# Late numerator sums added by a DMA, squares of six blocks added by GpSimd, in a kernel with an interleaved first phase

## The chip, the cores and the metric

One core of one Trainium2 chip. The metric is the device time of one execution in microseconds; the kernel before takes 4677.09 us (median of 3 runs, 4675.98 to 4685.37). In the text PE is TensorE, DVE is VectorE, ACT is ScalarE, POOL is GpSimd, and SP is the engine that only issues DMAs.

## The reference

Two layers over `x` of shape (4, 1024, 1024), float32. The part around the change is the first operation of each layer, a bidirectional decaying scan along the sequence, with the same `k = v = side` in both layers:

```python
decay = exp(-exp(w)) * (0.5 + 0.5 * tf)
ek = exp(minimum(k, 30)); ekv = ek * v
# a = a*decay + ekv, b = b*decay + ek, forward (nf, df) and backward (nb, db)
euk = exp(minimum(u + k, 30))
num = nf + nb - ekv + euk * v
den = df + db - ek + euk
out = sigmoid(r) * num / maximum(den, 1e-8) * (0.8 + 0.2 * tf)
```

Layer 0 then does `x + out @ (W * scale).T + bias`. Layer 1 adds its own scan result, and then an RMS norm (mean of squares over the 1024 channels), a router with the top 4 of 32 experts, a shared expert (`silu(h @ sg) * (h @ su) @ sd`) and the routed experts.

## The kernel before

The scans work on blocks: 128 channels (partitions) by 1024 positions. There are 32 blocks (4 batches of 8), and a **unit** is the work of one block for both layers, `l = 0` and `l = 1`. A unit leaves two tiles in DRAM: `gated` (layer 0, times sigmoid(x)) and `ratio` (layer 1).

The matmuls of layer 0, the norm and the shared expert work on **halves**: 512 positions of all 8 channel blocks. There are 8 halves, `h` = 0 to 7, of 32 **steps** each. A step is one 128-row product of 24 matmuls (operands are split in a high and a low float32r part, three matmuls per pair). Steps 0 to 15 make layer 0 and, in between, the down products of the half before; from step 16 on stand gate and up products. Between product 15 and product 16 lies the **normalisation**: every block has to be multiplied by the inverse root of the mean of squares before PE can go on.

The order is written out by hand in `with_halves`, the same for every engine. Units 0 to 7 run alone (while PE and ACT split the weights), and the last of them carries the first loads of half 0. After that half `h` (0 to 5) is interleaved with units 8+4h to 11+4h, eight steps in each: the unit calls `fill(0)` to `fill(7)` at its own places, and `fill` does what its engine has to do for that step. Halves 6 and 7 have no units. Then come the experts, a loop over some 150 tiles of 128 tokens, which is 57% of the span.

What the prediction follows, with lines of the kernel before:

- **Numerator.** DVE makes `W = min(euk, cap) * side` (L980), scans `G` forward (L972) and backward (L983). In units 0 to 7 PE adds the two in PSUM (L1421, L1426). In all later units DVE adds them, `G = G + W` (L988). DVE then makes the inverse in two Newton steps (L996, L998, both into `W`), multiplies (L1002, into `N`) and, for `l = 0`, multiplies by the sigmoid (L1007), which counts `gated` up.
- **The next unit's side tile.** ACT waits for `gated`, issues the store of `gated` (L719) and behind it, on the same queue, the load of the next unit's side tile (L665, `load_side`). When it has landed POOL clips it at 30 into `EK` (L595, `clip`, counts `kc`), and ACT takes the exponential (L660, `side_exp`), after `inverse(1)` and before `fill(6)`.
- **Squares.** ACT squares block `o` of the half into the one tile `SQ` (L785, at step `SQUARE_AT[o]`), and PE adds it up with a matmul against a tile of ones in `SUM_BANK` (L1467, at step `SUM_AT[o]`), 8 times per half. ACT can't write the next square before PE has read the last.
- **Steps 13 to 15.** PE transposes the half before's output block 4 into `OUT_BANK` (L1493), ACT copies it to `RS` (L768, in `fill(6)` of the second unit, right behind `side_exp`), SP stores `RS` (behind product 14, on which its queue waits), and only then can ACT copy block 5 (L768, `fill(7)`) and take logarithm and exponential of the sums (L793, L795). DVE refines the root (L1253 to L1261) and scales the first block (L1270), and PE starts the transposes of the normalisation (L1477). The transposes of output block 5 on PE wait for ACT's copy of block 4.

```python
SQUARE_AT = (3, 4, 5, 7, 9, 11, 13, 13)
SUM_AT = (5, 5, 6, 8, 10, 12, 13, 14)
COPY_AT = (6, 8, 10, 12, 14, 15, 17, 18)
R_AT = 2 * CB - 1
```

## Time and profile before

| | us |
|---|---|
| median of 3 runs (lowest, highest) | 4677.09 (4675.98, 4685.37) |
| span of the profiled execution | 4682.9 |
| PE busy | 4475.7 (96%) |
| DVE busy | 2567.2 (55%) |
| ACT busy | 1789.8 (38%) |
| POOL busy | 722.8 (15%) |

No time of the profiled execution is given besides its span, which is 5.8 us over the median of the runs. Busy time of PE is modelled: each matmul is shown longer than the distance to the next, so a PE that looks busy may still be paced by gaps; distances between starts are what the reader should take. Busy shares of the whole span mix five stages with different limits, so the stages are read one by one: the units alone (to about 311 us), half 0 up to its normalisation (to 404), the rest of the interleaved halves (to 1545), halves 6 and 7 (to 2003), and the experts.

### The profile page before, as it was taken

The numbers are of one execution on the slowest core, as the hardware profiler recorded it, in microseconds if no ns is written. First come the engines' busy times: TensorE is split into PE (matmuls) and PEld (weight loads), VectorE is DVE, ScalarE is ACT, GpSimd is POOL, SyncE is SP. The second block draws the span as 40 slices with busy tenths as digits, with TensorE's granted clock in tenths as the row PEclk, the third lists the DMA queues.
The fourth block names the chain that finished last, engine by engine and source line by source line (L and its number), as shares of the span: only waits on it lengthen the run. The fifth ranks groups of instructions, "written<-read, shape, count | busy, mean of one in ns | idle before, by whom it ended". The sixth has DMA issues, their size and how long they took to land.

```text
span 4682.9 us, 60901 instructions
## 1 busy us (share of the span) xinstructions
PE 4475.7 (96%) x19862; PEld 3545.7 (76%) x19863; DVE 2567.2 (55%) x2765; ACT 1789.8 (38%) x2596; POOL 722.8 (15%) x934
## 2 busy tenths in 40 slices
PE   6777999999999999999999999999999999999998
PEld 2245877777777877878888888888888888888887
DVE  8999999999999653433233434444341253333432
ACT  5665555555555333232222323334231142222321
POOL 1000000000000017211111112112111121111111
PEclk8888999999999999999999999999999999999999
DMA  6675767767676766754344545555552254444543
GB/s 226 235 263 184 274 241 268 251 223 282 240 268 226 270 212 190 251 182 111 95 131 112 170 112 160 171 166 150 182 168 57 61 186 145 112 112 116 161 109 61
DMA packets 247928, 835.08 MB, mean 178 GB/s; under 512 B 28160, under 2 KB 61056, under 8 KB 222976
## 3 DMA queue, kind: packets, MB, share of 16 engines
q1 hardware_dynamic: 172944, 572.77, 34.5%
q0 software_dynamic: 47728, 160.07, 15.5%
q10 hardware_dynamic: 27136, 100.67, 5.8%
q8 instruction: 72, 1.18, 0.1%
q14 instruction: 48, 0.39, 0.0%
HBM read 652.40 MB, written 181.01 MB: 178 GB/s over the span
## 4 chain that ended last, share of the span: by engine, by line
PE 80%; DVE 10%; issue 4%; ACT 3%; DMA 2%; POOL 0%; ACTq 0%; DVEq 0%; POOLq 0%; SPq 0%
PE ps L1593 34%; PE ps L1457 22%; PE ps L1607 16%; PE ps L1526 3%; PE ps L1479 1%; PE ps L1582 1%; DVE work L969 1%; DVE work L975 1%; DMA work<-rows_dram,row_idx 1%; PE ps L1477 1%; PE ps L1467 1%; DVE work L996 1%; DVE work L998 1%; DVE work L972 1%; DVE work L1002 1%
## 5 line engine op out<-in xcount | busy, mean ns | idle before, releaser
L1593 PE MATMUL ps<-halves 128*128 128x512 f32 x7152 | 1698.6, 393 | 3.5 <-DVE halves L1356 2.8
L1593 PEld LDWEIGHTS ps<-halves 128*128 128x128 f32 x7152 | 1338.5, 189 | 279.9 <-DVE halves L1356 3.1
L1457 PE MATMUL ps<-halves 128*128 128x512 f32 x6144 | 1450.2, 395 | 13.7 <-issue 12.5
L1457 PEld LDWEIGHTS ps<-halves 128*128 128x128 f32 x6144 | 1154.1, 189 | 287.2 <-issue 47.8
L1607 PE MATMUL ps<-halves 128*128 128x512 f32 x3576 | 834.9, 389 | 1.3 <-DVE halves L1372 1.3
L1607 PEld LDWEIGHTS ps<-halves 128*128 128x128 f32 x3576 | 671.1, 188 | 140.9 <-DVE halves L1372 1.6
L1356 DVE TENSOR_TENSOR halves<-ps,halves 128x1024 fp32r<-128x1024 f32 x150 | 183.7, 1225 | 905.2 <-ACT halves L852 905.2
L1351 DVE TENSOR_TENSOR halves<-work,halves 128x1024 fp32r<-128x1024 f32 (+1 forms) x320 | 440.2, 1433 | 83.6 <-ACT halves L856 83.3
L852 ACT ACTIVATE halves<-ps 128x1024 fp32r<-128x1024 f32 x150 | 154.0, 1027 | 862.4 <-PE ps L1593 862.4
L576 POOL DMA_INDIRECT out<-work,add_idx x149 | 249.8, 1677 | 1417.3 <-DVE work L1378 1382.2
L856 ACT ACTIVATE halves<-work 128x1024 fp32r<-128x1024 f32 (+1 forms) x320 | 369.1, 1229 | 67.0 <-PE ps L1607 56.5
L1372 DVE TENSOR_TENSOR halves<-ps,halves 128x256 fp32r<-128x256 f32 x298 | 112.4, 419 | 491.7 <-ACT halves L884 491.7
L595 POOL TENSOR_SCALAR work<-work 128x1024 f32<-128x1024 f32 x33 | 106.5, 3226 | 1419.9 <-DMA work<-side_t 1419.9
L884 ACT ACTIVATE halves<-ps 128x256 fp32r<-128x256 f32 x298 | 98.5, 382 | 544.4 <-PE ps L1582 544.4
L1378 DVE TENSOR_SCALAR work<-ps,acc 128x512 f32<-128x512 f32 x149 | 111.6, 749 | 276.4 <-PE ps L1607 266.5
L890 ACT ACTIVATE work<-ps,acc 128x512 f32<-128x512 f32 x149 | 102.1, 685 | 408.5 <-PE ps L1607 388.5
L566 POOL DMA_INDIRECT work<-rows_dram,row_idx x151 | 152.5, 1010 | 123.4 <-POOL row_idx L562 69.0
L1526 PE MATMUL ps<-ident,work 128*128 128x128 f32 x1200 | 157.6, 275 | 12.4 <-DMA work<-rows_dram,row_idx 12.4
L975 DVE TENSOR_TENSOR_SCAN work<-decay,edge_in,work 128x1024 f32<-128x1024 f32 x64 | 154.2, 2409 | 14.2 <-ACT edge_in L680 14.2
L1435 PE MATMUL ps<-plain,ident 128*128 128x512 f32 x128 | 83.0, 736 | 73.6 <-ACT halves L735 73.6
L983 DVE TENSOR_TENSOR_SCAN work<-decay,edge_in,work 128x1024 f32<-128x1024 f32 x64 | 150.7, 2355 | 0.0
L1526 PEld LDWEIGHTS ps<-ident,work 128*128 128x128 f32 x1200 | 137.1, 142 | 13.4 <-DMA work<-rows_dram,row_idx 13.3
(186 smaller groups left out, 3674.4 us busy)
## 6 DMA issues: line engine op xcount, KB each, us to landing
halves<-split_dram SPq DMA_DIRECT2D x512, 512.0 KB, 5.6
work<-expert_w SPq DMA_DIRECT2D x192, 1024.0 KB, 5.5
split_dram<-halves ACTq DMA_DIRECT2D x32, 1024.0 KB, 4.9
plain<-shared_w SPq DMA_DIRECT2D x32, 512.0 KB, 3.2
gated_dram<-work ACTq DMA_DIRECT2D x32, 512.0 KB, 4.1
work<-side_t ACTq DMA_DIRECT2D x32, 512.0 KB, 5.6
work<-x_t ACTq DMA_DIRECT2D x32, 512.0 KB, 3.7
ratio_dram<-work ACTq DMA_DIRECT2D x32, 512.0 KB, 4.2
```

Source lines behind the costliest of these rows:

```text
L566: pool.indirect_dma_start(hx, None, rows_dram[:, :], bass.IndirectOffsetOnAxis(row_idx[:, :].bitcast(u32), 0)).then_inc(s["rows_in"], 16)
L576: pool.indirect_dma_start(out[:, :], bass.IndirectOffsetOnAxis(add_idx[:, :].bitcast(u32), 0), y, None, compute_op=ALU.add).then_inc(s["y_ ...
L852: sc.activation(xhi, ps_xt[:, :], ACT.Copy).then_inc(s["x_hi"], 1)
L856: sc.activation(whi[q][:, part], staged(q, part), ACT.Copy).then_inc(s["w1_hi" if q < 4 else "w2_hi"], 1)
L975: ve.tensor_tensor_scan(F[:, ::-1], d, F[:, ::-1], edge_in[:, 0:1], ALU.mult, ALU.add).then_inc(s["h_bwd"], 1)
L983: ve.tensor_tensor_scan(G[:, ::-1], d, G[:, ::-1], edge_in[:, 1:2], ALU.mult, ALU.add).then_inc(s["nb"], 1)
L1351: ve.tensor_tensor(wlo[q][:, part], staged(q, part), whi[q][:, part].bitcast(f32), ALU.subtract)\
L1356: ve.tensor_tensor(xlo, ps_xt[:, :], xhi.bitcast(f32), ALU.subtract).then_inc(s["x_lo"], 1)
L1457: last = pe.matmul(bank(k % 4), w, op[:, part], start=(c == 0 and w is w_hi and op is hi), stop=(c == CB - 1 and w is w_lo))
L1526: last = pe.transpose(ps_xt[:, c * P:(c + 1) * P], hx[:, c * P:(c + 1) * P], ident[:, :])
L1593: last = pe.matmul(ps_h[:, a * 512:a * 512 + 512], xp[:, xk * P:(xk + 1) * P], wp[:, rhs], start=(xk == 0 and xp is xhi and wp is whi[q]), ...
L1607: last = pe.matmul(ps_y[:, h * 512:h * 512 + 512], ap_[:, (q * 2 + k) * P:(q * 2 + k + 1) * P], wp[:, rhs:rhs + 512], start=(q == 0 and k ...
```

## The change

1. `second`, three more tiles of 1024 columns, gives `W`, `F` and `G` one copy for each layer (`W_of[l]`, `F_of[l]`, `G_of[l]`). The Newton steps now write `F`, the product writes `W`, and `gated` and `ratio` are stored from there. `N` holds the inverse alone.
2. In units 8 to 31, but for 15, 23 and 31 (`prompt`), the numerator is added by a DMA that POOL issues, SBUF to SBUF with accumulation, 512 KB each, 42 in all. The product that needs it is made later (`scaled_late`): for `l = 0` behind the backward scan of `l = 1`, for `l = 1` in the next unit behind its first backward scan.
3. ACT's `store_gated`, with `load_side` in it, stands behind `fill(4)` and so behind the late product; the third and seventh `fill` come after the Newton steps on DVE, `fill(4)` between the scans of `l = 1`.
4. In halves 0 to 6 (`folded`) the square of block 0 goes to `R`, and POOL adds the squares of blocks 1 to 5 to it. PE sums three tiles: `R`, and the squares of blocks 6 and 7. Half 7 keeps its eight.
5. `SCRATCH`: the space for software DMA descriptors is 4096 bytes per partition instead of 16384.

```diff
+        second = sb("second", 3 * SEQ)
+        W_of, F_of, G_of = ((first, second[:, i * SEQ:(i + 1) * SEQ]) for i, first in enumerate((W, F, G)))
...
+        def prompt(u):
+            return u % CB == CB - 1
...
+            def add_numerator(u, l):
+                n = u * 2 + l
+                pool.wait_ge(s["wv_done"], n + 1)
+                pool.wait_ge(s["nb"], n + 1)
+                pool.dma_start(G_of[l], W_of[l], accum_op=ALU.add).then_inc(s["num_added"], 16)
+            def fold_square(h, o):
+                pool.wait_ge(s["sq"], h * CB + (o + 1))
+                if o > 1:
+                    pool.wait_ge(s["sq_folded"], h * (FOLDED - 1) + (o - 1))
+                apart(pool)
+                pool.tensor_tensor(R, R, SQ, ALU.add).then_inc(s["sq_folded"], 1)
...
+                if q == 1:
+                    fold_square(h, 4)
+                if not prompt(u):
+                    add_numerator(u, 0)
+                if q == 0:
+                    fold_square(h, 1)
+                    fold_square(h, 2)
+                if q == 1:
+                    fold_square(h, 5)
+                clip(u + 1, (u + 1) % 2)
+                if not prompt(u):
+                    add_numerator(u, 1)
+                if q == 0:
+                    fold_square(h, 3)
...
                 fill(2)
                 fill(3)
-                sc.wait_ge(s["gated"], u + 2)
-                sc.dma_start(gated_dram[ds(u * P, P), :], N).then_inc(s["gated_out"], 16)
-                load_side(u + 1, 1 - par)
-                fill(4)
+                if prompt:
+                    store_gated()
+                    fill(4)
                 edges(1)
                 euk(1)
+                if not prompt:
+                    fill(4)
+                    store_gated()
                 fill(5)
                 inverse(1)
                 side_exp(u + 1)
                 fill(6)
...
+                    if l == 1 and not prompt:
+                        fill(4)
                     ve.wait_ge(s["h_fwd"], n + 1)
                     ve.wait_ge(s["h_edge"], n + 1)
                     ve.tensor_tensor_scan(F[:, ::-1], d, F[:, ::-1], edge_in[:, 0:1], ALU.mult, ALU.add).then_inc(s["h_bwd"], 1)
+                    if l == 1 and not prompt:
+                        scaled_late(u, 0)
                     fill(4 * l + 1)
+                    if l == 0 and pending:
+                        scaled_late(u - 1, 1)
...
-                pe.matmul(SUM_BANK, ones[:, :], SQ, start=(o == 0), stop=(o == CB - 1)).then_inc(s["sums"], 1)
+                pe.matmul(SUM_BANK, ones[:, :], R if folded(h) and o == first else SQ, start=(o == first), stop=(o == CB - 1))\
+                    .then_inc(s["sums"], 1)
...
-    nc = bacc.Bacc("TRN2", target_bir_lowering=False, num_devices=1)
+    nc = bacc.Bacc("TRN2", target_bir_lowering=False, num_devices=1, dynamic_dma_scratch_size=SCRATCH)
```

How the order moves, at two places of the second unit of half 2 (the other halves read alike). On DVE before, from the second Newton step of `l = 0` to the backward scan of `l = 1` (L1002 is the product, L1007 the gated product, L1291 and L1298 belong to `fill(4)`):

```order
L998 SCALAR_TENSOR_TENSOR work<-work 128x1024 [waits newton1]
L1002 SCALAR_TENSOR_TENSOR work<-work,neg_gain 128x1024 [waits newton2]
L1007 TENSOR_TENSOR work<-work 128x1024 [waits sig_x,gated_raw]
L1291 TENSOR_TENSOR plain<-work 128x512 [waits rl_in0,sig1]
L1298 SCALAR_TENSOR_TENSOR work<-ps,lsb,work 128x512 [waits xl_in3,product]
L969 SCALAR_TENSOR_TENSOR work<-decay,work 128x1024
L972 SCALAR_TENSOR_TENSOR work<-decay,work 128x1024
L975 SCALAR_TENSOR_TENSOR work<-decay,edge_in,work 128x1024 [waits h_edge,h_fwd]
```

The same stretch in the changed kernel (L1080 is the second Newton step, L1048, L1051 and L1056 the scans, L1379 the `fill(3)` that stood before the Newton steps, L1027 and L1032 product and gated product):

```order
L1080 SCALAR_TENSOR_TENSOR work<-work 128x1024 [waits newton1]
L1379 SCALAR_TENSOR_TENSOR work<-ps,lsb,work 128x512 [waits xl_in2,product]
L1048 SCALAR_TENSOR_TENSOR second<-decay,work 128x1024 [waits newton2]
L1051 SCALAR_TENSOR_TENSOR second<-decay,work 128x1024
L1372 TENSOR_TENSOR plain<-work 128x512 [waits rl_in0,sig1]
L1379 SCALAR_TENSOR_TENSOR work<-ps,lsb,work 128x512 [waits xl_in3,product]
L1056 SCALAR_TENSOR_TENSOR second<-decay,edge_in,second 128x1024 [waits h_edge,h_fwd]
L1027 SCALAR_TENSOR_TENSOR work<-work,neg_gain 128x1024 [waits num_added]
L1032 TENSOR_TENSOR work<-work 128x1024 [waits sig_x,gated_raw]
```

The gated product has moved behind three scans and two `fill`s. On ACT before, from the store of `gated` to the logarithm of the sums (L665 loads the side tile, L660 is `side_exp`, L768 the copies of output blocks):

```order
L719 DMA gated_dram<-work 128x1024 [waits gated]
L665 DMA work<-side_t 128x1024 [waits gated]
...
L785 ACTIVATE work<-plain 128x512 [waits sums,c1] x2
L697 ACTIVATE work<-work,neg_low 128x1024 [waits h_all]
L704 ACTIVATE work<-work,low 128x1024 [waits den,gated_out]
L670 DMA work<-x_t 128x1024 [waits wv_done]
L708 ACTIVATE work<-work 128x1024 [waits g_ln]
L660 ACTIVATE work<-work 128x1024 [waits kc]
L768 ACTIVATE work<-ps 128x512 [waits o_out,o_tr] x2
L793 ACTIVATE work<-ps,eps 128x512 [waits sums]
```

And in the changed kernel (L723 loads the side tile, L718 is `side_exp`, L832 the copies, L862 the logarithm):

```order
L746 ACTIVATE second<-work,uu 128x1024 [waits ratio_out]
...
L750 DMA gated_dram<-work 128x1024 [waits gated]
L723 DMA work<-side_t 128x1024 [waits gated]
L854 ACTIVATE work<-plain 128x512 [waits sq_folded,c1]
L854 ACTIVATE work<-plain 128x512 [waits sums,c1]
L761 ACTIVATE second<-second,neg_low 128x1024 [waits h_all]
L764 ACTIVATE work<-second,low 128x1024 [waits den]
L728 DMA work<-x_t 128x1024 [waits wv_done]
L768 ACTIVATE work<-work 128x1024 [waits g_ln]
L718 ACTIVATE work<-work 128x1024 [waits kc]
L832 ACTIVATE work<-ps 128x512 [waits o_out,o_tr] x2
L862 ACTIVATE work<-ps,eps 128x512 [waits sums]
```

The load now stands behind the second `euk` and `fill(4)`; `side_exp` and the two copies behind it have kept their places.

## Rows read from the trace of the kernel before

**Rows 1.** Windows: length, busy us of PE, PEld, DVE, ACT, POOL; PEclk, DMA share, GB/s.
```profile
23.00:344.00 321.00, 233.86 (x491) 103.71 (x490) 293.72 (x187) 193.86 (x221) 28.52 (x9) 0.87 0.67 246
...
714.00:817.00 103.00, 100.12 (x434) 78.46 (x433) 97.62 (x87) 54.63 (x76) 5.54 (x2) 0.99 0.76 268
...
1647.00:1850.00 203.00, 200.15 (x873) 155.45 (x872) 84.87 (x142) 61.25 (x100) 88.18 (x91) 1.00 0.68 218
```

**Rows 2.** Timeline of PE in half 2: products, sums, the loop's turn.
```profile
748.90 6.05 PE L1457 MATMUL ps<-halves 128*128 128x512 f32 x24
754.79 1.02 PE L1467 MATMUL ps<-work,ones 128*128 128x512 f32 x2
755.24 6.05 PE L1457 MATMUL ps<-halves 128*128 128x512 f32 x24
...
840.61 76.42 PE L1457 MATMUL ps<-halves 128*128 128x512 f32 x336
920.09 4.14 PE L1457 MATMUL ps<-halves 128*128 128x512 f32 x10 [3.06 <-issue]
```

**Rows 3.** Timeline of PE before the normalisation of half 2, then half 6.
```profile
805.09 0.63 PE L1493 MATMUL ps<-ident,work 128*128 128x128 f32 x4 [0.28 <-ACT work L768]
...
814.77 1.11 PE L1477 MATMUL ps<-ident,work 128*128 128x128 f32 x4 [2.26 <-DVE work L1270]
...
1634.15 0.60 PE L1493 MATMUL ps<-ident,work 128*128 128x128 f32 x4
...
1644.37 1.11 PE L1477 MATMUL ps<-ident,work 128*128 128x128 f32 x4 [2.85 <-DVE work L1270]
```

**Rows 4.** Timeline of ACT in half 2, same place.
```profile
787.65 0.45 ACTq L665 DMA_DIRECT2D work<-side_t  x1
...
803.42 1.05 ACT L660 ACTIVATE work<-work 128x1024 f32<-128x1024 f32 x1
804.37 0.58 ACT L768 ACTIVATE work<-ps 128x512 f32<-128x512 f32 x1
809.59 0.60 ACT L768 ACTIVATE work<-ps 128x512 f32<-128x512 f32 x1 [4.64 <-DMA out<-work]
810.08 0.69 ACT L793 ACTIVATE work<-ps,eps 128x512 f32<-128x512 f32 x1
```

**Rows 5.** Timeline of POOL: clips of half 2, and of halves 1 and 5.
```profile
796.16 2.77 POOL L595 TENSOR_SCALAR work<-work 128x1024 f32<-128x1024 f32 x1 [46.05 <-DMA work<-side_t]
...
591.53 3.90 POOL L595 TENSOR_SCALAR work<-work 128x1024 f32<-128x1024 f32 x1 [46.98 <-DMA work<-side_t]
...
1421.40 2.83 POOL L595 TENSOR_SCALAR work<-work 128x1024 f32<-128x1024 f32 x1 [47.88 <-DMA work<-side_t]
```

**Rows 6.** Timeline of ACT: `side_exp` in halves 1 and 5.
```profile
596.37 1.04 ACT L660 ACTIVATE work<-work 128x1024 f32<-128x1024 f32 x1
...
1427.74 1.05 ACT L660 ACTIVATE work<-work 128x1024 f32<-128x1024 f32 x1
```

**Rows 7.** Timeline of DVE in half 2, second unit.
```profile
780.31 1.22 DVE L988 TENSOR_TENSOR work<-work 128x1024 f32<-128x1024 f32 x1
...
784.67 1.29 DVE L1002 SCALAR_TENSOR_TENSOR work<-work,neg_gain 128x1024 f32<-128x1024 f32 x1
786.00 1.23 DVE L1007 TENSOR_TENSOR work<-work 128x1024 f32<-128x1024 f32 x1
787.14 0.69 DVE L1291 TENSOR_TENSOR plain<-work 128x512 f32<-128x512 f32 x1
...
788.40 2.28 DVE L969 TENSOR_TENSOR_SCAN work<-decay,work 128x1024 f32<-128x1024 f32 x1
```

**Rows 8.** Timeline of DVE: a product beside a clip, and its next.
```profile
860.46 2.06 DVE L979 SCALAR_TENSOR_TENSOR work<-work,cap 128x1024 f32<-128x1024 f32 x1
862.44 1.27 DVE L980 SCALAR_TENSOR_TENSOR work<-work,cap 128x1024 f32<-128x1024 f32 x1
```

**Rows 9.** Waits of DVE in the units alone: us in total, times, longest.
```profile
DVE work L996 <- PE ps L1421: 6.5, 4, 1.8
```

More of the change, by code:

```diff
@@ L274, in scaled_gate, with added @@
             return h * STEPS + (CB + 2 * j + 1)
+        def prompt(u):
+            return u % CB == CB - 1
+        def added(u, l):
+            later = [v for v in range(ALONE, u) if not prompt(v)]
+            return 16 * (2 * len(later) + l + 1)
         PREP = 2 + 3 * BATCH
@@ L354, in with_halves @@
                 for par in range(2):
[L355 to L357 removed]
+                    unit(2 * v + par, par, lambda i: alone(2 * v + par, i), True, True, False)
+            last = ALONE - 1
+            unit(last - 1, 0, lambda i: alone(last - 1, i), True, True, False)
             def last_alone(i):
@@ L361, in last_alone @@
                 alone(last, i)
-            unit(last, 1, last_alone, True)
+            unit(last, 1, last_alone, True, True, False)
             for q in range(UNITS_PER_HALF):
-                unit(2 * UNITS_PER_HALF + q, q % 2, lambda i: fill(0, q * FILLS_PER_UNIT + i, first=True, prev=False, next_=True))
+                u = ALONE + q
+                unit(u, q % 2, lambda i: fill(0, q * FILLS_PER_UNIT + i, first=True, prev=False, next_=True),
+                     False, prompt(u), u > ALONE)
             for h in range(1, HALVES - 2):
                 for q in range(UNITS_PER_HALF):
-                    unit(h * UNITS_PER_HALF + (2 * UNITS_PER_HALF + q), q % 2,
-                         lambda i: fill(h, q * FILLS_PER_UNIT + i, first=False, prev=True, next_=True))
+                    u = h * UNITS_PER_HALF + ALONE + q
+                    unit(u, q % 2, lambda i: fill(h, q * FILLS_PER_UNIT + i, first=False, prev=True, next_=True),
+                         False, prompt(u), not prompt(u - 1))
             for h in range(HALVES - 2, HALVES):
@@ L468, in store_out, with unit @@
                 sp.dma_start(to, RS.rearrange("p (t c) -> p t c", c=P)).then_inc(s["o_out"], 16)
-            def unit(u, par, fill, summed_by_pe=False):
+            def unit(u, par, fill, summed_by_pe, prompt, pending):
                 for i in range(FILLS_PER_UNIT):
@@ L670, in load_x, with unit @@
                 sc.dma_start(x_of[par], x_t[ds(u % BLOCKS * P, P), :]).then_inc(s["x_in"], 16)
-            def unit(u, par, fill, summed_by_pe=False):
+            def unit(u, par, fill, summed_by_pe, prompt, pending):
                 fill(0)
@@ L783, in fill @@
                             sc.wait_ge(s["c1"], h * CB + (o + 1))
-                            wait(sc, "sums", h * CB + o)
-                            sc.activation(SQ, C1[o], ACT.Square).then_inc(s["sq"], 1)
+                            if folded(h) and o == 0:
+                                wait(sc, "z", h * CB)
+                            elif folded(h) and o <= FOLDED:
+                                wait(sc, "sq_folded", h * (FOLDED - 1) + (o - 1))
+                            else:
+                                wait(sc, "sums", squares_used(h, o - 1))
+                            sc.activation(R if folded(h) and o == 0 else SQ, C1[o], ACT.Square).then_inc(s["sq"], 1)
                     for o in range(CB):
@@ L954, in _, with scaled, scaled_late, unit @@
             ve.wait_ge(s["prep"], PREP + 9)
-            def unit(u, par, fill, summed_by_pe=False):
+            def scaled(u, l, par, num):
+                ve.scalar_tensor_tensor(W_of[l], num, neg_gain[:, ds(u, 1)], F_of[l], ALU.mult, ALU.mult)\
+                    .then_inc(s["gated_raw" if l == 0 else "ratio"], 1)
+                if l == 0:
+                    ve.wait_ge(s["gated_raw"], u + 1)
+                    ve.wait_ge(s["sig_x"], u + 1)
+                    ve.tensor_tensor(W_of[0], W_of[0], x_of[par], ALU.mult).then_inc(s["gated"], 1)
+            def scaled_late(u, l):
+                ve.wait_ge(s["num_added"], added(u, l))
+                scaled(u, l, u % 2, G_of[l])
+            def unit(u, par, fill, summed_by_pe, prompt, pending):
                 fill(0)
@@ L1420, in numerator @@
                     part = slice(j * HALF, (j + 1) * HALF)
-                    last = pe.matmul(NUM[:, part], ident[:, :], W[:, part], start=True, stop=False)
-                last.then_inc(s["num_w"], 1)
+                    pe.matmul(NUM[:, part], ident[:, :], W_of[l][:, part], start=True, stop=False)
                 pe.wait_ge(s["nb"], n + 1)
@@ L1425, in numerator @@
                     part = slice(j * HALF, (j + 1) * HALF)
-                    last = pe.matmul(NUM[:, part], ident[:, :], G[:, part], start=False, stop=True)
+                    last = pe.matmul(NUM[:, part], ident[:, :], G_of[l][:, part], start=False, stop=True)
                 last.then_inc(s["num"], 1)
```

94 lines of the change are left out of this document (54 added, 40 removed).

## The prediction

> **What bounds the kernel now.** The windows by stage come first [rows 1]. In the units alone DVE is busy 293.7 of 321 us while the clock of PE is granted at 0.87: DVE sets the pace there. In the interleaved halves PE shows 100.1 of 103 us and DVE 97.6, so the averages don't tell which one limits; in halves 6 and 7 DVE falls to 85 of 203 us and PE stays at 200. The second view is PE's timeline [rows 2]: fourteen products take 76.42 us, 5.46 us each, without a gap, in the middle of DVE's fullest stretch. DVE at 95% does not slow PE. PE has two gaps per half. One is 3.06 us at 920.09, put down to issue [rows 2]; it comes when PE's loop over halves turns, and none of the changed code touches it. The other stands before the normalisation: the transposes of half 2 start at 814.77, having waited 2.26 us for DVE [rows 3].
>
> The third view, and the one that decides, is what sets that moment. PE starts the last turn but one at 805.09 and waits 0.28 us for ACT's copy of output block 4 [rows 3]. In ACT's timeline [rows 4] that copy stands at 804.37, right behind `side_exp` at 803.42; the copy of block 5 waits 4.64 us for the store of block 4, and the logarithm follows at 810.08. So 11.35 us lie between the start of `side_exp` and the normalisation (814.77 - 803.42), with nothing in them that can shrink; PE waits for ACT there at both ends. In half 1 the same distance starts at 596.37 and in half 5 at 1427.74 [rows 6]; five halves have this pattern (half 0 has no copies of outputs). `side_exp` itself needs the clip, and the clip needs the side tile. Load issued at 787.65 [rows 4], clip 796.16 to 798.93 [rows 5]: 8.5 us of load, 2.8 us of clip, and then 4.5 us in which the clipped tile lies ready before ACT comes to it. In half 1 this slack is 596.37 - 595.43 = 0.9 us, in half 5 it is 1427.74 - 1424.23 = 3.5 us [rows 5, 6], and it averages 3.6 us over the five (halves 3 and 4, 5.3 and 3.6 us, read alike).
>
> **The change, part by part.**
>
> *Squares off PE.* A product with a square sum behind it takes 755.24 - 748.90 = 6.34 us, one without 5.46 [rows 2]: a sum costs 0.88 us. Five fall away per half, 4.4 us in each of halves 0 to 6. In half 6 the moment of normalisation follows PE: from the turn behind product 14 at 1634.15 to 1644.37 are 10.2 us [rows 3], the store of block 4 being queued on SP behind product 14. So half 6 should give **-4.4 us**. In half 0 PE waits for DVE up to its normalisation, and PE's work there is free. In halves 1 to 5 it is worth something only if ACT is in time, which is the question below.
>
> *Numerator sums off DVE.* 42 additions of 1.22 us [rows 7] leave DVE, 51 us in all, up to 9.8 us per half. PE did not wait for DVE's throughput, so by themselves they are worth nothing in halves 1 to 5. The DMAs move 512 KB each, as the side load does, which took 8.5 us with its queueing; the late product comes, by the retiming below, at 793 where the addition stood at 780, so I cost the DMA at nothing. The cover is 13 us; a DMA that takes longer makes DVE wait for the rest.
>
> *Squares on POOL.* POOL now runs 35 additions of two tiles of 128x512. The trace has none. The nearest row is the clip, one tile of 128x1024 in 2.77 us [rows 5], so a fold takes 1.4 to 2.8 us of POOL, which is idle. What it costs DVE shows beside a clip: L979 takes 2.06 us where its twin L980 takes 1.27 [rows 8], 0.8 us lost. I take 0.8 us per fold, 3.9 us per half; bounds are 0 and the whole 2.8 us. The Trainium skill (SBUF — State Buffer, "Who interferes with whom") says that a DVE instruction with two SBUF inputs and a GpSimd instruction that reads SBUF exclude each other for a whole instruction. The rows show 0.8 us and not the clip's 2.8; what the rule would make of the time is the third rival below.
>
> *The units alone.* Separate tiles take PE's read of `W` out of the Newton steps' way: those waits are 6.5 us [rows 9]. The product still waits for PE's second pair of matmuls, so I take **-4 us**, between 0 and -6.5.
>
> *The late product, and what hangs on it.* This is the step that I expect to cost. `load_side` waits for `gated`. Before, `gated` was one product away from the Newton steps. Now between them stand, on DVE: the moved `fill(3)` (one L1298, 0.7, which moved from ahead of them and cancels), three scans of 2.28, `fill(4)` at 788.40 - 787.14 = 1.3 [rows 7]. Ahead of them comes the late product of the unit before, 1.3, and the addition of 1.2 is gone. That is 6.8 + 1.3 + 1.3 - 1.2 = 8.2 us later. Two folds fall in the same stretch (+1.6), and DVE starts the unit earlier by what it saved in the first one, less three folds and a wait for ACT's sigmoid, which I put at 1.4 us (0 to 3). Sum: **8.4 us later**. The slack was 3.6 us on average, so `side_exp` starts 4.8 us later. ACT executes in order: the copies of blocks 4 and 5, the logarithm and the root stand behind it, and the normalisation moves by the same 4.8 us. PE, earlier by its 4.4 us, waits for block 4's copy that much longer. In five halves this is **+24 us**. Bounds: with the load at 5.5 us in place of 8.5, 2 us per half; with the slack of half 1 everywhere, 7.5 us per half: +10 to +37.
>
> The third units of a half lose similarly on ACT, but DVE needs the late tiles only after it has worked off its own Newton steps; the wait of some 4 us there is about what it saved. The first units have no copy in front of a normalisation behind them, prompt units are as before. Half 0's first two units: DVE saves 4.9 us, pays 3.9 us for folds, and has no copies behind `side_exp`: 0, within 3. The experts change in nothing but the descriptor space, which I cost at 0: POOL, which would wait for space, is busy for 15% of the span.
>
> Sum: -4 - 4.4 + 24 = +15.6 us on a span of 4682.9; the median of the runs is 5.8 us lower, so the forecast is 4677 + 16 = **4693 us**. Its own range: 4677 - 6.5 - 4.4 + 10 = 4676 to 4677 - 4.4 + 37 = 4710.
>
> **Rivals.**
>
> *ACT is in time, and it gets faster.* If the side tile came early enough, PE's saving would count in halves 1 to 5 as well, between 1 us (what DVE's own chain gains up to `inverse(1)`) and 4.4 us each: -4 - 4.4 - 5 to 22, so 4664 to 4647, say 4655. For it: DVE's relief is real, 9.8 us per half, and the moved work could begin earlier than I retime it. Against it: the load would have to be issued before 791, and by my retiming it is issued at 796. It decides when the delay of the load falls under the slack of 3.6 us.
>
> *Gain and loss cancel.* At 2 us per half the sum is -4 - 4.4 + 10 = +2, 4679 us. This needs shorter loads at their new place; nothing in the rows says so.
>
> *The folds hold DVE for their whole length.* With 2.8 us in place of 0.8 the five folds cost DVE 10 us more per half ahead of the normalisation; it has 5.4 us to spare per 103 [rows 1], so some 5 us per half more in five halves: 4693 + 25 = 4718. The clip rows speak against it, though a fold reads two tiles and not one.
>
> **How the numbers follow.** Differences within 0.2%, 9.4 us, are about what a measurement of this kernel can't tell from no change. The forecast has 0.56, the faster rival 0.22, the cancelling one 0.15, held folds 0.07. The low end of the forecast's own range falls within 0.2%, so slower by more than that has 0.60, faster 0.22, same 0.18. The range takes in the upper part of the faster rival and most of the forecast's bounds: 4652 to 4712.
>
> **What would show it.** In the profile after: L718 waiting for POOL's clip by 3 to 7 us in the second units of halves 1 to 5 (before, the tile lay ready); PE's turn before product 15 waiting for ACT's copy by some 8 us; some 5 us more between two normalisations up to that of half 5, and 4 us less from there to that of half 6; three square sums per half on PE; DVE about 45 us less busy. I am wrong if L718 does not wait, or if it waits and the normalisation is not later; if DVE waits for `num_added`; or if folds lengthen DVE's instructions by more than 1 us each.

## The result and the profile after

The changed kernel takes 4688.2 us (median of 20 runs, 4680.5 to 4693.0) against 4679.1 us for the kernel before in the same session: a ratio of 1.0018, with a 95% interval of 1.0012 to 1.0025. It is slower by 9.1 us. Forecast were 16 us more than before, 4693 us. The difference lies just inside the 0.2% that the prediction had set as the bound of "same", and clearly outside zero.

First the page of the changed kernel: the busy times, and the queue that carries the new accumulating DMAs.

```profile
PE 4445.5 (95%) x19792; PEld 3536.4 (76%) x19793; DVE 2538.4 (54%) x2723; ACT 1792.1 (38%) x2596; POOL 834.6 (18%) x1011
...
q0 software_dynamic: 53776, 182.09, 17.7%
```

PE is busy 30.2 us less and DVE 28.8 us less than in the table of before, POOL 112 us more. The queue moved 160.07 MB before, so the 42 accumulating DMAs are the 22 MB that came on top. Both of the loaded engines lost work, and the kernel became slower. The windows say where to look; columns as in [rows 1], and the first two stretches are the same as there.

```profile
23.00:344.00 321.00, 243.88 (x557) 113.93 (x556) 299.90 (x191) 197.72 (x225) 32.48 (x12) 0.88 0.67 249
...
714.00:817.00 103.00, 95.41 (x401) 76.89 (x401) 90.96 (x74) 52.67 (x72) 22.38 (x11) 0.93 0.83 274
```

In the interleaved stretch PE's busy time falls from 100.1 to 95.4 us of 103, and DVE from 97.6 to 91.0. Neither bounds the stretch; both wait more. In half 2 this is the place on ACT, beside [rows 4]:

```profile
797.42 0.44 ACTq L723 DMA_DIRECT2D work<-side_t  x1
...
803.05 1.06 ACT L768 ACTIVATE work<-work 128x1024 f32<-128x1024 f32 x1
808.74 1.06 ACT L718 ACTIVATE work<-work 128x1024 f32<-128x1024 f32 x1 [4.62 <-POOL work L620]
809.70 0.58 ACT L832 ACTIVATE work<-ps 128x512 f32<-128x512 f32 x1
815.98 0.60 ACT L832 ACTIVATE work<-ps 128x512 f32<-128x512 f32 x1 [5.70 <-DMA out<-work]
816.47 0.68 ACT L862 ACTIVATE work<-ps,eps 128x512 f32<-128x512 f32 x1
```

The load of the side tile, `side_exp` (L718), the two copies (L832) and the logarithm (L862) are the instructions of [rows 4] in the same order. `side_exp` now waits 4.62 us for the clip. The clip, beside [rows 5], and PE, beside [rows 3]:

```profile
805.27 3.43 POOL L620 TENSOR_SCALAR work<-work 128x1024 f32<-128x1024 f32 x1 [20.34 <-DMA work<-side_t]
```

```profile
798.52 0.60 PE L1580 MATMUL ps<-ident,work 128*128 128x128 f32 x4
...
799.41 6.03 PE L1537 MATMUL ps<-halves 128*128 128x512 f32 x24
810.42 1.09 PE L1580 MATMUL ps<-ident,work 128*128 128x128 f32 x4 [4.98 <-ACT work L832]
811.30 1.92 PE L1553 MATMUL ps<-work,ones 128*128 128x512 f32 x2
812.23 7.96 PE L1537 MATMUL ps<-halves 128*128 128x512 f32 x24
```

PE waits 4.98 us for ACT's copy, and the product behind the wait takes 7.96 us where the one ahead of it takes 6.03. While PE stood, its granted clock fell, to about the lower of its two levels:

```profile
810.40:817.00 6.60, 6.58 (x17) 4.76 (x18) 1.44 (x2) 1.02 (x2) 0.00 (x0) 0.56 0.53 112
```

From 799.00 to 805.40 it is 1.00, and before the change it is 1.00 from 806 to 812, where the same product runs behind a wait of 0.28 us. Over halves 1 to 5 the product behind this wait takes 6.1, 8.0, 7.7, 6.9 and 6.0 us, so a wait can cost PE up to 2 us beside its own length. In half 2 that is nearly all hidden: the normalisation then waits another 0.42 us for DVE. One more thing stands in these rows, and I had not used it: PE's turn of block 4 is over at 799.1, but ACT's copy of block 4 runs at 809.70. Its input lay ready for 10.6 us. Experiment 6 rests on that.

The waits from 404 to 1545 us, halves 0 to 5 (us in total, times, longest):

```profile
ACT work L718 <- POOL work L620: 79.8, 19, 5.9
ACT work L832 <- DMA out<-work: 67.2, 15, 6.9
...
PE ps L1580 <- ACT work L832: 34.1, 11, 6.4
DVE work L1334 <- ACT work L862: 23.4, 5, 5.6
```

No wait of DVE for `num_added` stands among them. The account by stages is taken from DVE's timeline, from the start of the root of each half (L1253 before, L1334 after):

| root of half | 0 | 1 | 2 | 3 | 4 | 5 | 6 | 7 |
|---|---|---|---|---|---|---|---|---|
| before, us | 400.1 | 604.6 | 811.0 | 1020.2 | 1227.9 | 1436.2 | 1640.6 | 1844.1 |
| after, us | 394.6 | 605.6 | 817.3 | 1026.9 | 1236.7 | 1446.4 | 1644.2 | 1848.1 |
| after less before | -5.5 | +1.0 | +6.3 | +6.7 | +8.8 | +10.2 | +3.6 | +4.0 |

Halves 1 to 5 lose 6.5, 5.3, 0.4, 2.1 and 1.4 us, 15.7 in all; half 6 gives back 6.6. Up to the last root the profiled execution is 4.0 us behind. Its whole span is 4679.8 us, which is even 3.1 us under that of before; the medians say +9.1. So 5 us of the difference have no place that one pair of traces could show. The profiled execution of the changed kernel took 4681.5 us, 6.7 us less than its median and the second fastest of the 20, while the one of before lies above its median: differences of this size are taken from the medians, and the traces say where, not how much.

### The profile page after: what moved, and what is told of

Same layout as the page of the kernel before. It is cut to its first block, busy times and chain, and to the rows that moved or that the text cites. A ratio compares the mean times of both kernels' runs of the same rounds, so it can differ in the third digit from the quotient of the medians.

```text
span 4679.8 us, 60797 instructions
## 1 busy us (share of the span) xinstructions
PE 4445.5 (95%) x19792; PEld 3536.4 (76%) x19793; DVE 2538.4 (54%) x2723; ACT 1792.1 (38%) x2596; POOL 834.6 (18%) x1011
## 3 DMA queue, kind: packets, MB, share of 16 engines
q8 instruction: 68, 1.11, 0.1%
## 4 chain that ended last, share of the span: by engine, by line
PE 72%; DVE 9%; DMA 4%; issue 4%; ACT 1%; POOL 1%; ACTq 0%; POOLq 0%; DVEq 0%; SPq 0%
PE ps L1680 34%; PE ps L1694 16%; PE ps L1537 16%; PE ps L1613 3%; DMA work<-side_t 2%; PE ps L1669 1%; PE ps L1566 1%; DMA work<-rows_dram,row_idx 1%; POOL work L620 1%; DVE second L1056 1%; DMA out<-work 1%; PE ps L1564 1%; DVE second L1048 1%; DVE work L1027 1%; DVE halves L1432 0%
## 5 line engine op out<-in xcount | busy, mean ns | idle before, releaser
L1537 PE MATMUL ps<-halves 128*128 128x512 f32 x6144 | 1443.6, 395 | 11.4 <-issue 10.5
L611 POOL DMA_INDIRECT slots_dram<-acc x128 | 126.1, 986 | 111.4 <-DVE acc L1195 73.1
L586 POOL COPY acc<-work (+1 forms) x151 | 49.3, 326 | 479.9 <-PE ps L1613 465.7
```

Source lines behind the costliest of these rows:

```text
L611: pool.indirect_dma_start(slots_dram[:, :], bass.IndirectOffsetOnAxis(where[:, t * TOPK + k:t * TOPK + k + 1].bitcast(u32), 0), entry[:, 2 ...
L1537: last = pe.matmul(bank(k % 4), w, op[:, part], start=(c == 0 and w is w_hi and op is hi), stop=(c == CB - 1 and w is w_lo))
```

## The experiments

Twelve runs, in three sessions, of 5 to 12 executions each. The chips of these sessions give 4812 us for the kernel before, some 133 us more than the first one, in every kernel at the same place in half 7 (shown in the last section). The changed kernel was run again there and has the same ratio, 1.0016. All comparisons are by ratio to before, or in us between runs of these sessions; where an expectation names us, they are on the base of the first session, 4679 us. "Roots 1 to 5" is the distance between the roots of half 1 and half 5 in DVE's timeline: 831.6 us before and 840.7 after in the first session, 843.4 for the changed kernel run again.

**1. `exp_behind`: the late tile may stay late, but the normalisation no longer stands behind it.**

```
-                side_exp(u + 1)
+                behind = not summed_by_pe and u % UNITS_PER_HALF == 1
+                if not behind:
+                    side_exp(u + 1)
                 fill(6)
                 fill(7)
+                if behind:
+                    side_exp(u + 1)
```

> The changed kernel with one ACT instruction moved: in the second unit of each half the exponential of the next side tile (`side_exp`) is issued behind the copies of output blocks 4 and 5, the logarithm and the root, and no longer ahead of them. The late side tile stays late. Theory (the late side tile holds up ACT, and the normalisations stand behind ACT): the normalisations of halves 1 to 5 no longer wait for it; the 15.7 us that they lost come back, and some of PE's 4.4 us per half beside: 4655 to 4672 us, and PE's wait for ACT's copy before the last product of a half is gone. Rival 1 (the folds' load on DVE is the cost) and rival 2 (DVE's new order itself is the cost): ACT's order matters little, 4683 to 4693 us.

Measured: 0.9998 (0.9989 to 1.0007), 4812.6 us, 8 us under the changed kernel (4678 us on the first base, between the two expectations). Roots 1 to 5: 835.0 us. The rival that ACT's order does not matter is out, but only a part of what I expected came back. PE no longer waits for the copy of block 4 ahead of the last product, and that product runs at a clock of 1.00. ACT in half 2:

```profile
809.04 0.58 ACT L836 ACTIVATE work<-ps 128x512 f32<-128x512 f32 x1
816.62 0.60 ACT L836 ACTIVATE work<-ps 128x512 f32<-128x512 f32 x1 [7.00 <-DMA out<-work]
817.11 0.68 ACT L866 ACTIVATE work<-ps,eps 128x512 f32<-128x512 f32 x1
817.83 0.63 ACT L868 ACTIVATE work<-work 128x512 f32<-128x512 f32 x1
818.36 1.04 ACT L718 ACTIVATE work<-work 128x1024 f32<-128x1024 f32 x1
```

and SP:

```profile
799.91 10.94 SPq L421 DMA_DIRECT2D halves<-split_dram  x4
810.90 0.43 SPq L493 DMA_DIRECT2D out<-work  x1
```

`side_exp` (L718) is behind the root's exponential (L868) now. But the copy of block 5 waits 7.00 us for the store of block 4, which SP issues at 810.90, behind loads of pieces that wait for PE. In the changed kernel the store is issued 0.02 us behind the end of copy 4, here 1.24 to 1.28 us behind it in halves 1 to 5; from issue to the copy of block 5 it takes 5.6 to 5.7 us in halves 2 to 5 here, and 5.0 to 6.7 in the changed kernel. From copy 4 to the root's exponential are 8.7 to 8.8 us in halves 2 to 5 and 10.8 in half 1, where the changed kernel has 6.9 to 8.5, or 7.4 to 8.8 when run again, and the kernel before 5.8 to 7.5. So with `side_exp` out of the way the store waits in SP's queue, behind loads that wait for PE's product, and PE stands 3.70 us for DVE before each of the five normalisations.

**2. `second_prompt`: the second unit of each half as before the change.**

```
-            return u % CB == CB - 1
+            return u % CB == CB - 1 or u % UNITS_PER_HALF == 1
```

(and the count of the sums on DVE and the flag of a pending product, which follow from it)

> The changed kernel with the second unit of each half made prompt (its two sums on DVE as before, `gated` right behind the Newton steps); the other units stay late, the squares stay folded. Theory (late side tile): the load is issued some 8 us earlier, the tile lies ready, the normalisations of halves 1 to 5 come back by 15.7 us, and a part of PE's 4.4 us per half shows: 4655 to 4674 us. Rival 1 (folds): all of them are still there, and DVE has 14 sums more: 4688 us or up to 10 more. Rival 2 (late sums as such, in all units): a third of the loss comes back, about 4683 us.

Measured: 0.9998 (0.9989 to 1.0007), roots 1 to 5 836.3 us. It is 9 us under the changed kernel, more than the third that rival 2 gives and less than the theory says. Making a unit prompt takes back the order of DVE and ACT along with the addition, so this run does not separate the two. The late second unit is where more than half of the loss comes from.

**3. `no_fold`: the squares back on PE, the late sums kept.**

```
         def folded(h):
-            return not final(h)
+            return False
         def squares_used(h, o):
-            return h * (CB - FOLDED + 1) + (o + 1 if final(h) else o - FOLDED + 2)
+            return h * CB + o + 1
```

(and no `fold_square` on POOL)

> The changed kernel with all eight squares of a half summed by PE again and no additions by POOL; the late numerator sums stay. Theory (late side tile): in halves 1 to 5 PE has 4.4 us more to do but waited for ACT by about as much (34 us over 11 waits), DVE is freed of some 2 us ahead of `gated`, half 6 loses 4.4 us: 4682 to 4694 us. Rival 1 (the folds' load on DVE is the cost of the change): 35 folds with 1.0 us each go, 4660 to 4675 us. Rival 3 (PE sets the pace all the same): 4.4 us more in each of seven halves, 4715 to 4720 us.

Measured: 1.0022 (1.0012 to 1.0032), 4822.5 us, 2 us over the changed kernel, with intervals that overlap. Roots 1 to 5 841.5 us. The 35 folds are neither the cost of the change nor, in this order, a gain in halves 1 to 5. The time is inside the range of the theory. Half 5 to 6 takes 202.8 us here, and with folds 197.8 in the changed kernel and 196.6 when run again: there they are worth 5 to 6 us, as it should be where PE sets the pace.

**4. `all_prompt`: no late sums, the folds kept.**

```
         def prompt(u):
-            return u % CB == CB - 1
+            return True
```

> The changed kernel without any late sum: every unit is prompt, no accumulating DMA is issued; the folded squares and the second set of tiles stay. Theory (late side tile): the side tile is on time again, the normalisations of halves 1 to 5 come back by 15.7 us, and part of PE's 4.4 us per half shows: 4655 to 4674 us. Rival 1 (the folds are the cost): they are all there, and DVE has its 51 us of sums back: 4688 to 4710 us.

Measured: 0.9984 (0.9975 to 0.9993), 4805.0 us, roots 1 to 5 828.2 us. Against the changed kernel that is 15 us less, and 1.0016 and 0.9984 have intervals far apart. So the late sums, with the order that they bring, cost 15 us, though they take 51 us of work from DVE. Against before it is a gain of 8 us, 4672 us on the first base, at the small end of what the theory gave.

**5. `after_again` and `all_prompt_no_fold`: the measure, and what is left without both.** The second has the edits of `all_prompt` and `no_fold` together.

> The changed kernel itself, as the measure for the runs beside it on this chip: 1.0018 of the time of before, 0.1% either way.

> The changed kernel without late sums and without folded squares: of the change only the second set of tiles, the order of the stores and the smaller descriptor space are left. Theory (separate tiles help the units alone and nothing else): 0.9982 to 0.9995 of before. If the folds are worth something once the late sums are gone, this stands above the run without late sums (0.9984) by 4 to 16 us; rival (the folds cost DVE what they save PE): the two are the same.

Measured: 1.0016 (1.0007 to 1.0024), 4820.4 us, for the changed kernel, and 0.9977 (0.9968 to 0.9986), 4802.5 us, without late sums and folds. Of the whole change, then, the second set of tiles (with what came along: the order of the stores and the descriptor space) is a gain of 10 us. That is more than the range that I had given (0.9982 to 0.9995); 5.5 us of it stand at the root of half 0 already (394.6 in place of 400.1), the place of the rest is not shown. The folds added to it lose 2.5 us, which the intervals don't tell from nothing. DVE's busy time prices a fold: 2591.1 us with folds and 2567.8 without, 23.3 us over 35, 0.67 us each; with the late sums 2536.9 and 2513.2, 0.68 us.

**6. `copy_early`: one number of a table, against the copy that lies ready for 10 us.**

```
-COPY_AT = (6, 8, 10, 12, 14, 15, 17, 18)
+COPY_AT = (6, 8, 10, 12, 13, 15, 17, 18)
```

> The changed kernel with one number of a table: the copy of output block 4 moves on ACT from step 14 to step 13, ahead of the second unit's last inverse and of `side_exp` (its store on SP follows by a step). Theory (what sets the normalisation is ACT's copy of block 4 behind the inverse and `side_exp`, its store, its landing and the copy of block 5): the copy runs some 5 us earlier, and the normalisations of halves 1 to 5 come 3 to 5 us earlier each: 0.9965 to 0.9990 of before, 15 to 25 us under the changed kernel. Rival (DVE's work up to the normalisation sets it, and ACT's copies only ride along): no difference from the changed kernel.

Measured: 0.9938 (0.9925 to 0.9950), 4782.1 us. It is 38 us faster than the changed kernel and 30 us faster than before, and the first version that beats both by a clear margin. I had expected 15 to 25, so the range was missed on the good side. The number moves the copy on ACT and, one step behind it, its store on SP. Roots 1 to 5: 819.5 us. ACT in half 2, and DVE's root:

```profile
793.78 0.60 ACT L832 ACTIVATE work<-ps 128x512 f32<-128x512 f32 x1 [3.31 <-PE ps L1580]
...
801.66 1.06 ACT L718 ACTIVATE work<-work 128x1024 f32<-128x1024 f32 x1 [1.45 <-POOL work L620]
802.62 0.58 ACT L832 ACTIVATE work<-ps 128x512 f32<-128x512 f32 x1
803.10 0.68 ACT L862 ACTIVATE work<-ps,eps 128x512 f32<-128x512 f32 x1
```

```profile
803.53 0.75 DVE L1387 SCALAR_TENSOR_TENSOR work<-work,lsb,plain 128x512 f32<-128x512 f32 x1
804.20 0.69 DVE L1334 TENSOR_SCALAR work<-ps 128x512 f32<-128x512 f32 x1
```

The copy of block 4 waits for its input and not the input for it. The store lands while ACT computes the inverse, so the copy of block 5 starts without a wait for a DMA. And PE comes to the normalisation of half 2 straight from its last product:

```profile
802.26 6.05 PE L1537 MATMUL ps<-halves 128*128 128x512 f32 x24
808.58 0.60 PE L1564 MATMUL ps<-ident,work 128*128 128x128 f32 x4
```

The same holds in all of halves 1 to 5, where PE waited for DVE by 2.3 to 3.2 us before the change, and by 0.4 to 3.7 us in the changed kernel. PE sets the pace there now. In halves 0 to 5 the waits of L832 for stores fall from 67.2 to 31.9 us:

```profile
ACT work L718 <- POOL work L620: 69.9, 16, 5.3
ACT work L832 <- DMA out<-work: 31.9, 10, 7.1
```

`side_exp` waits nearly as much as in the changed kernel. Its lateness was not the whole matter; what counted was how much stood behind it.

**7. `all_prompt_copy` and `before_copy`: is the early copy a gain by itself?** The edit of 6, on the kernel of 4 and on the kernel before.

> No late sums, and the copy of output block 4 at step 13. Theory (copy 4, store, landing, copy 5 is the chain ahead of the normalisation): 3 to 5 us per half under the run without late sums, 0.993 to 0.996 of before. Rival (DVE sets it): 0.998, as without the move.

> The kernel before with the copy of block 4 at step 13 and nothing else. Theory (the early copy pays only where DVE is ahead; without late sums the copy at step 13 waits on ACT for the store of block 3 and for the turn, and holds back what stands behind it, as in the run without late sums, which lost 4 us by it): 0.999 to 1.002. Rival (the early copy is a gain by itself, of 5 us per half): 0.993 to 0.996.

Measured: 0.9993 (0.9984 to 1.0002) without late sums, 0.9995 (0.9986 to 1.0004) on the kernel before. The early copy alone is worth nothing in the sum. By the roots it is a gain and a loss: half 5 to 6 takes 199.4 us (before 204.4) and 194.2 without late sums (197.7 with the late copy), and from the root of half 0 to that of half 5 the first takes 5.8 us more and the second 10.3 (by single traces of different sessions). My expectation for the first of the two fell; the second, written after it, held. Why, ACT and DVE of `before_copy` show in half 2:

```profile
803.10 0.60 ACT L768 ACTIVATE work<-ps 128x512 f32<-128x512 f32 x1 [4.28 <-DMA out<-work]
...
811.34 0.60 ACT L768 ACTIVATE work<-ps 128x512 f32<-128x512 f32 x1 [0.83 <-PE ps L1493]
812.20 0.69 ACT L793 ACTIVATE work<-ps,eps 128x512 f32<-128x512 f32 x1 [0.27 <-PE ps L1467]
812.92 0.63 ACT L795 ACTIVATE work<-work 128x512 f32<-128x512 f32 x1
```

```profile
812.12 0.75 DVE L1306 SCALAR_TENSOR_TENSOR work<-work,lsb,plain 128x512 f32<-128x512 f32 x1
812.79 1.28 DVE L996 SCALAR_TENSOR_TENSOR work<-work,low 128x1024 f32<-128x1024 f32 x1
814.10 1.22 DVE L998 SCALAR_TENSOR_TENSOR work<-work 128x1024 f32<-128x1024 f32 x1
815.36 1.28 DVE L1002 SCALAR_TENSOR_TENSOR work<-work,neg_gain 128x1024 f32<-128x1024 f32 x1
816.56 0.68 DVE L1253 TENSOR_SCALAR work<-ps 128x512 f32<-128x512 f32 x1
```

The root's exponential (L795) starts at 812.92, but DVE reaches its part of the root at 816.56, 3.6 us later: its two Newton steps and the product of the second unit stand in front. In all of halves 1 to 5 this lag is 3.6 to 3.7 us in `before_copy` and in `all_prompt_copy`; in `copy_early` it is 0.1 to 0.5 us. The reason is DVE's order and not the addition that is gone. In a prompt unit the two Newton steps and the product (1.28 + 1.22 + 1.28 us) stand behind `fill(7)`, which waits for PE's last product ahead of the normalisation; in a late unit the Newton steps stand ahead of it, at 800.36 and 801.67 in `copy_early`, and the product stands behind the root. The addition stands ahead of `fill(7)` in `before_copy`, at 808.62, and behind it DVE waits 1.55 us for PE. DVE takes the place of ACT as the last to come. On ACT, too, the early copy waits 4.28 us for the store of block 3 here (first row).

**8. `second_prompt_copy`: late or prompt second unit, with the copy early.** The edits of 2 and 6 together.

> The run with early copy, and the second units prompt. Theory (once the copy is out of the way the late sums pay: they take work from DVE ahead of the second units' last `h_all`, which is what the copies and the inverse wait for): slower than with late second units, 0.995 to 0.998 of before. Rival (the late second unit costs by its late side tile, as forecast): faster, 0.989 to 0.993.

Measured: 0.9997 (0.9988 to 1.0006), 29 us slower than `copy_early`, and beyond the range of the theory. The rival is out. The lag of DVE at the root is back at 3.6 us, roots 1 to 5 are 841.6 us. So the sign of the late second unit turns with the place of one copy: +9 us with the copy at step 14, -29 us with it at step 13. The same for the late sums as a whole: +15 us at step 14 (4 against `after_again`) and -26 us at step 13 (4808.0 to 4782.1 us). The rows of experiment 7 point to the new order on DVE as what pays here, 3.2 to 3.6 us of lag in each of five halves; that is argued and not tested, since a kernel with this order and the additions still on DVE was not run. What the DMAs themselves are worth is open.

**9. `copy_early_no_fold`: the folds, with the copy early.** The edits of 3 and 6 together.

> Late sums, the copy of block 4 at step 13, and all eight squares summed by PE. Theory (with the copy out of the way PE sets the pace, its waits are down to 7 us per half, so its work is worth its time): 3 to 4.4 us per half more in halves 1 to 6, 18 to 27 us over the run with early copy (0.9938): 0.9975 to 1.0000 of before. Rival (the folds cost DVE ahead of the normalisation as much as they save PE, as it looked without the early copy, where taking them away cost 2 us): 0.993 to 0.995.

Measured: 0.9951 (0.9938 to 0.9965), 4789.9 us, 8 us over `copy_early`, between the two expectations and at the edge of the rival's (0.993 to 0.995). The trace is clearer than the medians: roots 1 to 5 take 829.5 us in place of 819.5, and half 5 to 6 199.5 in place of 194.5. Up to the root of half 6 the folds are worth 1626.1 - 1614.7 = 11.4 us, where without the early copy they were worth next to nothing in halves 1 to 5. That goes with the rows of experiment 6: PE's work is worth its time where PE no longer waits before the normalisation.

**10. `copy_early_exp`: the edits of 1 and 6 together.**

> The run with early copy, and `side_exp` of the second units behind the logarithm and the root. Theory (the late side tile still holds up ACT, 70 us over 16 waits, but only the part in front of a normalisation counts: 1.45 us of it in half 2): 0 to 1.5 us per half, 0.992 to 0.994 of before. Rival (the late tile is the whole rest of the loss): 3 or more us per half, 0.990 or less.

Measured: 0.9933 (0.9919 to 0.9946), 4780.6 us. Against `copy_early` that is 1.5 us, which the intervals don't tell from nothing. With the copy early the late side tile costs nearly nothing.

Not tried: the new order on DVE with the additions left there, the descriptor space alone, and a second staging tile for the output copies.

## Why the prediction came out as it did

The direction, the mechanism and the place were right, the size was not, and one step of the argument was wrong without harm to the number. That the median came out at +9.1 us is in part luck: up to the last root the traces show +4.0, which is nearer to the +2 of the rival "gain and loss cancel" than to the forecast's +16.

- *Units alone, -4 us.* The ninth unit starts at 305.8 us, before at 311.8: **-6.0**, near the bound of 6.5. The wait of [rows 9] for PE is gone.
- *Half 0, 0 within 3 us.* The root of half 0 is 5.5 us earlier, so it kept the 6 us of the units alone. Right.
- *Load of the side tile 8.4 us later.* Measured from the exponential of the root before it, the load of the second unit is issued at 193.9, 191.9, 191.6, 192.0 and 191.3 us in halves 1 to 5; before at 186.0, 184.5, 186.1, 183.9 and 184.0. That is **7.2 us later** on average, 1.2 short of the forecast.
- *`side_exp` 4.8 us later in each of five halves.* This is the term that was mis-sized. `side_exp` starts 3.4, 2.9, -0.7, 1.0 and 0.4 us later, **1.4 on average**. I had kept the load at 8.5 us. From issue to clip it took 9.0 us on average before and takes 6.7 after. These 2.3 us and the 1.2 of the line above are the 3.4 us that were missing. I had named that case as the lower bound and held nothing in the rows for it.
- *11.35 us from `side_exp` to the normalisation, with nothing that can shrink.* It did not shrink, it grew: from copy 4 to the root's exponential are 5.8 to 7.5 us before and 6.9 to 8.5 after, **1.0 us more** per half. It lies in the store between the two copies: from its issue to the copy of block 5 are 4.7 us on average before and 5.9 after, while its issue came 0.2 us sooner. And the sentence was wrong as a statement on the code: the copy need not stand there, and moving it by one step, with its store, is worth 38 us. I had read the chain of what waits for what, and had not asked of each link when its input was ready.
- *Sum for halves 1 to 5.* Forecast +24, measured +15.7: 12 us by the two terms above, and 3.6 us which DVE had gained in half 0 (its root came 4.4 us behind ACT's exponential before and 0.8 after), and gives back in half 1, where it waits for ACT.
- *Half 6, -4.4 us.* **-6.6**. Experiment 3 gives 5.0 us of it to the folds, 1 us per square sum and not 0.88.
- *A fold costs DVE 0.8 us.* 0.67 and 0.68 us by busy time, 0.84 with the early copy. Right on average. A fold of 1.52 us beside an instruction of DVE that takes 1.22 us alone:

```profile
734.04 1.22 DVE L1080 SCALAR_TENSOR_TENSOR work<-work 128x1024 f32<-128x1024 f32 x1
...
782.51 1.27 DVE L1078 SCALAR_TENSOR_TENSOR work<-work,low 128x1024 f32<-128x1024 f32 x1
783.82 2.20 DVE L1080 SCALAR_TENSOR_TENSOR work<-work 128x1024 f32<-128x1024 f32 x1
```

```profile
783.41 1.52 POOL L635 TENSOR_TENSOR work<-work 128x512 f32<-128x512 f32 x1 [1.22 <-ACT work L854]
```

DVE loses 0.98 us here. The fold starts at 783.41 under the first Newton step (L1078), which runs on to 783.78, and ends at 784.93, 1.11 us after the start of the second step (L1080): that step lost about what was left of the fold. The Trainium skill (SBUF — State Buffer, "Who interferes with whom") has the two exclude each other for a whole instruction, and these rows agree with it within 0.13 us. For a clip the rows don't. Before the change this one runs to 863.18:

```profile
859.92 3.26 POOL L595 TENSOR_SCALAR work<-work 128x1024 f32<-128x1024 f32 x1 [60.98 <-DMA work<-side_t]
```

L979 of [rows 8] starts 0.54 us behind it, loses 0.8 us and ends at 862.52, inside the clip, and its next loses nothing. So the price of 0.8 us that I took from the clip was met on average, but a single fold cost next to nothing or about 1 us in most cases, by the instruction that it fell beside. POOL pays more than DVE: the mean over the 35 folds is 2.2 us, with single ones of 3.03 and 4.42 us, and 1.26 to 1.52 where it fared best. The one of 3.03 us starts under a scan that runs to 745.01 and ends 1.09 us behind it.

```profile
L635 POOL TENSOR_TENSOR work<-work 128x512 f32<-128x512 f32 x35 | 76.9, 2198 | 224.8 <-ACT work L854 224.7
...
742.67 2.34 DVE L1056 TENSOR_TENSOR_SCAN second<-decay,edge_in,second 128x1024 f32<-128x1024 f32 x1
...
743.07 3.03 POOL L635 TENSOR_TENSOR work<-work 128x512 f32<-128x512 f32 x1 [10.82 <-ACT work L854]
...
776.96 4.42 POOL L635 TENSOR_TENSOR work<-work 128x512 f32<-128x512 f32 x1 [12.85 <-ACT work L854]
```

- *DVE about 45 us less busy.* 28.8 less: 51 us of sums, less some 23 us for the folds. I had not carried my own 0.8 us per fold into that line.
- *The rivals.* "ACT in time" did not happen. With the copy out of the way (experiment 6) the kernel does get faster, by 30 us against before, the far end of the 13 to 30 us that this rival gave, but not by the rival's condition: the side tile is late there too (69.9 us of waits). "Gain and loss cancel" had the load's length right: its mechanism, shorter loads, took 2.3 us per half off the forecast, 11.5 in five halves, of which the longer stores and what DVE gave back took some again; the result lies between it and mine. "Folds hold DVE" is out by experiment 3.
- *The signs I had listed.* In the second units of halves 1 to 5 `side_exp` waits 3.2, 4.6, 3.0, 2.2 and 1.8 us for the clip (I said 3 to 7), and PE's turn before the last product 3.6, 5.0, 3.3, 2.5 and 2.2 us for the copy (I said some 8): both weaker than forecast, and at the end of the row outside it. The longest waits of the two lines in the list above, 5.9 and 6.4 us, stand at other places. Three square sums per half stand on PE, and DVE never waits for `num_added`. The accumulating DMAs are hidden, as forecast.

What stays open: 5 of the 9.1 us between the medians would have to lie behind the last root, where the one pair of traces shows the opposite sign. Why the side tile's load got shorter and the output's store longer is not shown either. And the late sums were never run without the order that came with them.

## What to carry to other kernels

Work taken from two busy engines is worth nothing while a third, with half its time idle, has one instruction standing in the wrong place of its order: ask of every link of the chain in front of a join when its input was ready, not only what it waited for. And test a change together with the order around it: here the late sums cost 15 us in the given order, the folds changed nothing in halves 1 to 5, and the early copy changed nothing on the kernel before, while all three together are 30 us faster than before, 10 of which the second set of tiles has without them. Tried one by one, each of the three would have been thrown out.

## What the runs showed of the hardware

**PE slow while POOL issues indirect DMAs.** In the three later sessions every profiled kernel loses some 130 us in half 7 (328 to 333 us between its last two roots, in place of 204), while POOL issues its indirect DMAs one after another. PE of `after_again` there:

```profile
1775.42 0.58 PE L1537 MATMUL ps<-halves 128*128 128x512 f32 x1 [2.22 <-issue]
1778.22 0.59 PE L1537 MATMUL ps<-halves 128*128 128x512 f32 x1 [2.22 <-issue]
```

One matmul every 2.80 us, with 2.2 us in which PE waited for nothing that the profile shows. The same stretch as windows, `after_again` first and the changed kernel of the first session second:

```profile
1760.00:1890.00 130.00, 29.27 (x55) 14.46 (x53) 2.83 (x4) 2.70 (x4) 94.58 (x99) 0.51 0.11 29
```

```profile
1760.00:1890.00 130.00, 126.65 (x553) 95.76 (x552) 44.49 (x76) 39.63 (x65) 94.66 (x96) 1.00 0.68 208
```

POOL does the same work in both (94.6 us), but 29 GB/s move in place of 208, and PE's granted clock is 0.51, about the lower of its two levels. The kernel before its change has it too (`before_copy`, 104 us of waits put down to issue in PE's row from 1560 to 1960), so the change has no part in it. That POOL's DMAs are the cause is not shown, only that the two stand at the same time; what makes the chips differ was not looked into.

**An addition on POOL and a two-input instruction on DVE took turns.** A fold that starts under a scan or a Newton step ends 1.1 to 1.2 us behind that instruction, and the next two-input instruction of DVE takes about 1 us longer (2.20 us for 1.22, and 2.25 for 1.25 at 744.93). A clip of 128x1024 cost DVE 0.8 us of its 2.8.

**PE's clock fell in a wait of 5 us.** Behind the wait of 4.98 us the granted clock is 0.56 and the product takes 7.96 us for 6.03; behind one of 0.28 us it is 1.00.

**Loads late in a unit were shorter.** The same 512 KB load with its queueing took 9.0 us from issue to clip, and 6.7 us when issued 7.2 us later, although the core moved more by DMA in that stretch (274 GB/s in the window above, 268 in [rows 1]). In the changed kernel run again it is 6.4 us. Why is not shown.
